# Twelve weight loads issued at once, an unrolled output stage, and a gate table built earlier, in a graph network and mixture-of-experts kernel

## What is computed

```python
# x: (1250, 512), gate_weight: (16, 512), w1: (16, 256, 512), w2: (16, 512, 256), TOP_K = 2
gate_logits = x @ gate_weight.T
top_vals, top_idx = jax.lax.top_k(gate_logits, TOP_K)
routing_w = jax.nn.softmax(top_vals, axis=-1)
mask = jnp.any(top_idx[:, :, None] == jnp.arange(E)[None, None, :], axis=1)
h = jax.nn.silu(jnp.einsum('td,efd->tef', x, w1))
counts = jnp.sum(mask, axis=0)
h_sum = jnp.einsum('tef,te->ef', h, mask.astype(h.dtype))
h_mean = h_sum / jnp.maximum(counts, 1)[:, None]
y_mean = jnp.einsum('ef,edf->ed', h_mean, w2)
y_mean = jnp.where((counts > 0)[:, None], y_mean, 0.0)
out = jnp.einsum('tk,tkd->td', routing_w, y_mean[top_idx])
```

## Time and profile before

| what | us |
| --- | --- |
| median of 3 runs | 1175.64 (1173.95 to 1177.01) |
| profiled execution, whole time | 1175.32 |
| its span in the profile | 1173.7 |
| PE busy over the span | 1059.8 (90%) |
| DVE busy | 969.4 (83%) |
| ACT busy | 839.6 (72%) |
| POOL busy | 668.8 (57%) |

### The profile page before, as it was taken

The page is one execution under the profiler, slowest core; times in us unless marked ns, Lnnn a source line. Parts: engine busy times, 40 slices in busy tenths (PEclk is TensorE's granted clock), DMA queues, the critical chain, the costliest instruction groups (busy, mean ns, idle before and its releaser), DMA issues. The chain is left out here.

```text
span 1173.7 us, 19190 instructions
## 1 busy us (share of the span) xinstructions
PE 1059.8 (90%) x5670; PEld 882.1 (75%) x5670; DVE 969.4 (83%) x1646; ACT 839.6 (72%) x1028; POOL 668.8 (57%) x522
## 2 busy tenths in 40 slices
PE   2993999999999999999999999999569997599974
PEld 1772788888888888888888888888347776589962
DVE  6751699999999999999999999999857878773366
ACT  3212799999999999999999999999435454344442
POOL 3245777877877877777777877883321211044310
PEclk9996999999999999999999999999779999789975
DMA  6736766666666666666666666663020311635445
GB/s 179 258 113 147 153 132 131 135 131 133 135 130 131 140 131 131 129 137 131 127 131 133 137 132 126 133 131 101 1 73 10 125 35 53 225 91 152 146 133 170
DMA packets 129067, 148.77 MB, mean 127 GB/s; under 512 B 72573, under 2 KB 81158, under 8 KB 128893
## 3 DMA queue, kind: packets, MB, share of 16 engines
q0 software_dynamic: 38576, 97.54, 38.6%
q1 hardware_dynamic: 90381, 50.03, 16.0%
q10 hardware_dynamic: 16, 0.02, 0.0%
HBM read 137.00 MB, written 15.66 MB: 130 GB/s over the span
## 5 line engine op out<-in xcount | busy, mean ns | idle before, releaser
L944 PE MATMUL ps<-W2h,w1l_w3l 128*128 128x512 f32 x1264 | 425.8, 398 | 0.0
L794 POOL DMA_INDIRECT gath<-dst_table,idx_sl x158 | 262.8, 1663 | 54.0 <-issue 47.4
L944 PEld LDWEIGHTS ps<-W2h,w1l_w3l 128*128 128x128 f32 x1264 | 227.1, 189 | 38.1
L944 PE MATMUL ps<-W2l,w1l_w3l 128*128 128x512 f32 x632 | 247.3, 391 | 0.0
L807 POOL DMA_INDIRECT gath<-src_table,idx_sl x156 | 188.2, 1206 | 100.8 <-issue 52.4
L816 POOL TENSOR_TENSOR msg_lo<-act,msg_hi 128x512 fp32r<-128x512 f32 x79 | 126.0, 1595 | 35.5 <-DVE msg_hi L928 35.5
L944 PEld LDWEIGHTS ps<-W2l,w1l_w3l 128*128 128x128 f32 x632 | 118.8, 188 | 26.4
L878 DVE TENSOR_TENSOR agg<-agg,ps 125x512 f32 x166 | 114.1, 688 | 15.2 <-PE ps L988 10.7
L833 ACT ACTIVATE act<-ps 128x1024 f32<-128x1024 f32 x79 | 81.2, 1027 | 38.4 <-PE ps L976 38.4
L908 DVE SCALAR_TENSOR_TENSOR act<-act,ps 128x1024 f32<-128x1024 f32 x79 | 96.0, 1215 | 2.8 <-ACT act L861 2.8
L890 DVE SCALAR_TENSOR_TENSOR act<-act,ps 128x1024 f32<-128x1024 f32 x79 | 96.0, 1215 | 2.1 <-ACT act L852 2.1
(11 more groups left out here) (345 smaller groups left out, 2363.7 us busy)
## 6 DMA issues: line engine op xcount, KB each, us to landing
w_raw<-in_L_ffn_w_dram SPq DMA_DIRECT2D x25, 512.0 KB, 4.6
ea_sl<-ea_scr SPq DMA_DIRECT2D x158, 64.0 KB, 4.2
ea_scr<-in_edge_attr_dram POOLq DMA_DIRECT2D x1, 5000.0 KB
w_late<-in_L_ffn_w_dram SPq DMA_DIRECT2D x7, 512.0 KB, 6.3
w_raw<-in_L_gnn_W_dram SPq DMA_DIRECT2D x3, 1024.0 KB, 11.5
gath<-src_table,idx_sl POOLq DMA_INDIRECT x158
gath<-dst_table,idx_sl POOLq DMA_INDIRECT x158
x_raw<-in_x_dram SPq DMA_DIRECT2D x5, 448.0 KB
```

Of the source, the lines that this page charges most:

```text
L794: pool.indirect_dma_start(out=gath[:, k, j, :], out_offset=None, in_=dst_table[:, :], in_offset=bass.IndirectOffsetOnAxis(ap=idx_sl[:, p % ...
L944: return nc.tensor.matmul(ps_2[:, p % 2, j, :], part[:, p % 2, d, j * P:(j + 1) * P], weights[:, d, :], start=False, stop=last)
```

## The change

Of w2, twelve matrices get buffers of their own, `w2_more`, in the memory of all of w1T, which is free once the routed loop's last multiplication is done. SP waits for that (`h_ps` = RT) and issues the twelve loads one behind the other. The output stage is written out for all 16 experts on ACT, PE and DVE. DVE writes its sums straight into `yT`, with two halves of `xg` for the unused products, so the copy and the wait for its own last four go.

The table `gw3` becomes two tensors outside w1T, `gw3a` (8 blocks) and `gw3b` (2 blocks). POOL fills them with zeros at the start of the phase, behind the index tables. PE transposes `gw` in three parts at the ends of turns 4, 6 and 14 of the routed loop, ACT rounds each part twice at turns 6 to 9, 16 and 17, and DVE takes the low parts at turns 10, 12 and 20. POOL's zeros for `y3` now wait for `hm`. At the end SP writes out the even blocks and ACT the odd ones.

```diff
+GATES_AT, UPPER_AT, LOWER_AT = (4, 6, 14), (6, 7, 8, 9, 16, 17), (10, 12, 20)
...
+        ROWS, GWB = 2 * 32 + E, 8
+        gw3a = sb("gw3a", [ROWS, GWB * NB + NE - NB], F32R)
         sb("w1T_room", [P, (T["w1T_at"] - nc.sbuf_base) // 4 + E * 2 * KC * FFN])
+        gw3b = sb("gw3b", [ROWS, (BLOCKS - GWB) * NB + NE - NB], F32R)
+        w2_more = nc.alloc_sbuf_tensor_at("w2_more", [P, E - WS, KC, FFN], F32, offset=T["w1T_at"])
...
+        GW_PARTS = (range(0, 4), range(4, GWB), range(GWB, BLOCKS))
+        def gw_ps_part(n):
+            return (ps_b, ps_m, ps_b)[n][0:E, 0:len(GW_PARTS[n]) * NB]
...
@@ sync
-                need(sp, S["y_step"], (e - (WS - 1)) * KC)
-                sp.dma_start(w2_raw[:, k], w2_rows[bass.ds(e, 1)].rearrange("a p q f -> (a p) q f")).then_inc(w2_in[k], 16)
-            steps(sp, load_w2, 0, E - 1, WS, E - 1, WS)
-            for t in range(BLOCKS):
+            sp.wait_ge(S["h_ps"], RT)
+            for e in range(WS, E):
+                sp.dma_start(w2_more[:, e - WS], w2_rows[e]).then_inc(w2_in[e], 16)
+
+            for t in range(0, BLOCKS, 2):
...
@@ gpsimd
             nc.gpsimd.memset(hsum[:], 0.0).then_inc(S["const"], 1)
+            for part in (gw3a, gw3b):
+                nc.gpsimd.tensor_scalar(part[:], ones[0:ROWS, 0:1].to_broadcast(list(part.shape)), 0.0, None, ALU.mult).then_inc(S["gw_zeroed"], 1)
...
-            pool.wait_ge(S["h_ps"], RT)
-            for part in (gw3, y3):
-                nc.gpsimd.tensor_scalar(part, ones[0:ROWS, 0:1].to_broadcast(list(part.shape)), 0.0, None, ALU.mult).then_inc(S["out_zeroed"], 1)
-            pool.wait_ge(S["gw3_hi"], 2)
-            nc.gpsimd.tensor_tensor(gw3[64:64 + E, 0:NODES], gwT[:], f32(gw3[0:E, 0:NODES]), ALU.subtract).then_inc(S["gw3_lo"], 1)
+            pool.wait_ge(S["hm_ready"], 1)
+            nc.gpsimd.tensor_scalar(y3, ones[0:ROWS, 0:1].to_broadcast(list(y3.shape)), 0.0, None, ALU.mult).then_inc(S["out_zeroed"], 1)
@@ scalar
+                if t in UPPER_AT:
+                    part, half = divmod(UPPER_AT.index(t), 2)
+                    act.wait_ge(S["gw_zeroed"], 2)
+                    act.wait_ge(S["gw_ps"], part + 1)
+                    nc.scalar.activation(gw3_part(part, 32 * half), gw_ps_part(part), ACT.Copy).then_inc(S["gw_hi"], 1)
...
-            steps(act, diagonal, 0, E - 1, WS, E - 1, WS)
-
-            act.wait_ge(S["out_zeroed"], 2)
-            act.wait_ge(S["gw_out"], 3)
-            for r in (0, 32):
-                nc.scalar.activation(gw3[r:r + E, 0:NODES], gwT[:], ACT.Copy).then_inc(S["gw3_hi"], 1)
...
+            for t in range(1, BLOCKS, 2):
+                act.wait_ge(S["res_done"], t + 1)
+                for rows in ROW_PARTS:
+                    act.dma_start(out[t * NB + rows.start:t * NB + rows.stop, :], x1_all[rows, t, :]).then_inc(S["odd_out"], 16)
+            act.wait_ge(S["odd_out"], 32 * (BLOCKS // 2))
@@ vector
+                if t in LOWER_AT:
+                    part = LOWER_AT.index(t)
+                    dve.wait_ge(S["gw_hi"], 2 * part + 1)
+                    nc.vector.tensor_tensor(gw3_part(part, 64), gw_ps_part(part), f32(gw3_part(part, 0)), ALU.subtract).then_inc(S["gw3_lo"], 1)
...
-            steps(dve, output, 0, E, WS, E - 1, WS)
+            for e in range(E):
+                dve.wait_ge(w2_in[e], 16)
+                dve.wait_ge(S["mean_ps"], e + 1)
+                need(dve, S["y_step"], (e - 1) * KC)
+                for q in range(KC):
+                    nc.vector.tensor_tensor_reduce(out=junk_y[:, e % 2, q, :], in0=w2_tile(e)[:, q, :], in1=ps_n[:, e % 2, 0:FFN], scale=1.0, scalar=0.0,
+                                                   op0=ALU.mult, op1=ALU.add, accum_out=yT[:, q, e:e + 1]).then_inc(S["y_step"], 1)
@@ tensor
+                if t in GATES_AT:
+                    part = GATES_AT.index(t)
+                    pe.wait_ge(S["gw_ready"], 1)
+                    if part == 2:
+                        pe.wait_ge(S["gw_hi"], 2)
+                        pe.wait_ge(S["gw3_lo"], 1)
+                    for k, b in enumerate(GW_PARTS[part]):
+                        ins = nc.tensor.transpose(gw_ps_part(part)[:, k * NB:(k + 1) * NB], gw[:, b, :], ident[0:NB, 0:NB])
+                    ins.then_inc(S["gw_ps"], 1)
...
-            steps(pe, means, 0, E - 1, WS, E - 1, WS)
-
-            pe.wait_ge(S["y_done"], E)
+            pe.wait_ge(S["y_step"], E * KC)
```

More of the change, by code:

```diff
@@ L1548, in flat, with w2_tile, gw3_part, gw3_block @@
             return ap.rearrange("p a b -> p (a b)")
+        def w2_tile(e):
+            return w2_raw[:, e] if e < WS else w2_more[:, e - WS]
+        GW_PARTS = (range(0, 4), range(4, GWB), range(GWB, BLOCKS))
+        def gw_ps_part(n):
+            return (ps_b, ps_m, ps_b)[n][0:E, 0:len(GW_PARTS[n]) * NB]
+        def gw3_part(n, r):
+            tile, first = (gw3a, 0) if n < 2 else (gw3b, GWB)
+            return tile[r:r + E, (GW_PARTS[n].start - first) * NB:(GW_PARTS[n].stop - first) * NB]
+        def gw3_block(t):
+            tile, first = (gw3a, 0) if t < GWB else (gw3b, GWB)
+            return tile[:, (t - first) * NB:(t - first) * NB + NE]
         @block.sync
@@ L1556, in _ @@
                 sp.dma_start(w1_late[:, e - EARLY - WS, 1], w1_rows[e]).then_inc(w1_in[e - EARLY - WS], 16)
[L1558 to L1564, removed]
-                need(sp, S["y_step"], (e - (WS - 1)) * KC)
-                sp.dma_start(w2_raw[:, k], w2_rows[bass.ds(e, 1)].rearrange("a p q f -> (a p) q f")).then_inc(w2_in[k], 16)
-            steps(sp, load_w2, 0, E - 1, WS, E - 1, WS)
-            for t in range(BLOCKS):
+            for e in range(WS):
+                sp.wait_ge(S["w1T_ps"], (E - EARLY) * FC)
+                sp.wait_ge(S["h_ps"], RT * (e + 1) // (WS + 1))
+                sp.dma_start(w2_raw[:, e], w2_rows[e]).then_inc(w2_in[e], 16)
+            sp.wait_ge(S["h_ps"], RT)
+            for e in range(WS, E):
+                sp.dma_start(w2_more[:, e - WS], w2_rows[e]).then_inc(w2_in[e], 16)
+            for t in range(0, BLOCKS, 2):
                 sp.wait_ge(S["res_done"], t + 1)
                 for rows in ROW_PARTS:
-                    sp.dma_start(out[t * NB + rows.start:t * NB + rows.stop, :], x1_all[rows, t, :]).then_inc(S["res_out"], 16)
-            sp.wait_ge(S["res_out"], 32 * BLOCKS)
+                    sp.dma_start(out[t * NB + rows.start:t * NB + rows.stop, :], x1_all[rows, t, :]).then_inc(S["even_out"], 16)
+            sp.wait_ge(S["even_out"], 32 * (BLOCKS // 2))
         @block.gpsimd
@@ L1874, in means @@
                 for f in range(FC):
-                    ins = nc.tensor.matmul(ps_n[:, k, f * P:(f + 1) * P], ones[:], spread_hm[:, k, f, :], start=True, stop=True)
+                    ins = nc.tensor.matmul(ps_n[:, e % 2, f * P:(f + 1) * P], ones[:], spread_hm[:, e % 2, f, :], start=True, stop=True)
                 ins.then_inc(S["mean_ps"], 1)
-            steps(pe, means, 0, E - 1, WS, E - 1, WS)
-            pe.wait_ge(S["y_done"], E)
+            pe.wait_ge(S["y_step"], E * KC)
             for q in range(KC):
@@ L1890, in _ @@
                 ps = (ps_t[0:NE, t % 2, :], ps_s[0:NE, t % 2, :])[t // 2 % 2]
[L1891 removed]
+                nc.tensor.matmul(ps, gw3_block(t), y3, start=True, stop=True).then_inc(S["res_ps"], 1)
 _INS = ["x", "src", "dst", "edge_attr_64", "L0_gnn_W1", "L0_gnn_b1", "L0_gnn_W2", "L0_gnn_b2", "L0_gnn_W3", "L0_gnn_b3",
```

53 lines of the change are left out of this document (10 added, 43 removed).

## The result

| | before | after |
| --- | --- | --- |
| median, us | 1176.18 (1173.95 to 1177.80, 5 runs) | 1169.22 (1167.95 to 1171.46, 5 runs) |
| span of the profiled execution | 1173.7 | 1168.0 |

The ratio is 0.9942 (95% interval 0.9927 to 0.9957), which is 6.8 us of 1176.18; the two medians lie 7.0 apart. Forecast was a gain of 5.7, to a median of 1169.9.

A forecast was written before the change was run, and what follows sets the result against it. PE bounds the routed loop; the output stage behind it, 29.54 us, holds the largest prize. +2.3 +1.1 -1.5 -6.0 -1.6 = -5.7 us, from 1175.64 to a median of 1169.9, range 1166.6 to 1173.0.

The forecast's parts named there:

- Output stage: Behind the loop: self-wait, copy and loop instructions go, two experts need 2.94 us, the stage 23.55 against 29.54, gain 6.0.
- Rival 2: Output stage: the step stays near 1.65 us, a gain of 3 rather than 6, time 1172.9; chance 0.17.
- `hm`: Behind the loop: no POOL instruction runs before `hm` now, so it takes about 0.18 us, a gain of 1.5.
- The loads: Twelve w2 matrices, 6.29 MB, start when the last multiplication ends; all land early, at no cost.
- Rival 3: Output stage: the load burst starves engines of code; the gain of 5.7 becomes a loss of 3.5 us; chance 0.05.
- Gate table in the loop: Routed loop: ten transposes cost PE, the bound, their full 1.1 us; slack of 1.17 us covers ACT's six instructions.
- The end: Output writes: with half the issues on ACT, issuing no longer paces the end, a gain of 1.6 us.
- Zeros in routing: Start of routing: POOL's two fills hold DVE's chain, 2.2 us by the first and 0.1 by the second, costing 2.3.
- it was let go some 0.53 ahead: Start of routing: DVE's first instruction, held like `hm`, is let go 0.53 us before the fill's end, 2.2 late.
- Rival 1: Start of routing: POOL's fills don't hold DVE, the term of 2.3 us is 0, time 1167.6; chance 0.13.
- The sum: Whole kernel: all the gains and costs together make -5.7 us, for a median of 1169.9.

The follow-up runs named there:

- the edit of the kernel before: The kernel before, with POOL's two fills behind the loop waiting for `hm` instead of the last multiplication: median 1173.29 us, ratio 0.9980.

## Why the prediction was right, and where it was not

- **Output stage (-6.0).** Right, -6.03, and by its mechanism: bank handover 2.93 us for two experts against 2.94 forecast, confirmed by the third bank (22.01) and the self-wait (26.06). Rival 2 (a step that stays near 1.65) did not come.
- **`hm` (-1.5).** Right, -1.48. That POOL held it, which the prediction inferred from two rows, is shown by the edit of the kernel before.
- **The loads (0).** Right: no wait, the last bytes moved by 1147. Rival 3, engines short of code behind the burst, did not come: no row of the output stage shows such a wait.
- **Gate table in the loop (+1.1).** Right: 1.1 between the kernels with the table in and behind the loop, which is PE's part alone, so nothing is left for ACT's six instructions. A later turn takes 2.32 us, as forecast; the first ones were longer, by the clock.
- **The end (-1.6).** Right, -1.60, and 1.5 given back with one queue.
- **Zeros in routing (+2.3).** The step that failed: "it was let go some 0.53 ahead" of the fill's end was carried from one fill to another with other columns. The fill of 1001 columns held DVE for 0.8 and not for 2.2 us. The prediction also took from the Trainium skill, page "SBUF — State Buffer", section "Who interferes with whom", that DVE has to wait for the GpSimd instruction; the measurement decides, and here DVE passed from 0.9 us into a fill of 2.75 on. What the prediction did not have at all is the second part: the delay moves PE's work, and PE is granted 1.2 GHz at the loop's start. Against the kernel with memset the sum is 2.2 (0.9 in routing, 0.3 to the loop, 1.3 in it, less 0.3 behind it). So the term's size was nearly met for a wrong reason, which is luck. Rival 1, no hold, was wrong too.
- **The sum.** -5.7 forecast, -6.8 measured, -6.5 from T0 in the profiles. The 0.8 between forecast and profiles lies before the loop: routing grew by 1.3 and not 2.3, of which 0.9 is the hold and 0.4 the clock of the counts, and the way to the loop by 0.3. The second part of the fills' price doesn't show in this pair, since the profile of before had its loop on the slower level itself (82.83, against 81.37 in three other kernels with the same loop). Against a kernel before with slow counts and the faster loop, as in those three, the gain would be 162.23 + 0.42 - 1.46 - 155.71 = 5.5 us, an estimate from the table. Which levels the timed runs of the kernel before had no profile shows.

## What to carry to other kernels

Before a piece of work is moved to an idle engine, look at what the busy one does at the same moment: POOL had time for a fill that reads SBUF, but the fill held VectorE on the critical path, and memset did the same fill without that. Where two engines hand a pair of banks to and fro, add the handovers to both ends' times; a third bank gave the slower engine its own pace back. And put work that TensorE must do where it waits, not where it is the bound, even if that is a later stage.

## What the runs showed of the hardware

- POOL's `tensor_scalar` fills held DVE in parts of their time only: in the first 0.9 us of 2.75 with 1001 columns, and from 1.4 or earlier to 2.9 of 3.42 us with 1251 columns. POOL's memset (0.93 us) didn't hold it.
- A delay of 1 us on DVE, some 30 us before the loop, cost TensorE's full clock at the loop's start, and with it 2 us, whether POOL or three small instructions made it. The profile of before lost it there without the delay.
- Twelve loads of 512 KB, issued by SP one behind the other, moved 348 GB/s; SP needed 14.1 us to issue them, although one alone was issued in 0.37 us.
